# A grouped convolution and a routed low-rank layer on one core: two early tiles in shared blocks, and another order of VectorE's work

## What is computed

```python
out = lax.conv_general_dilated(x, weight, ..., feature_group_count=GROUPS)
out = out + ctx[:, :, None] + bias[None, :, None]        # ctx = c @ c_weight.T
...
base_out = einsum('btd,od->bto', x, base_W) + base_b
probs = softmax(einsum('btd,nd->btn', x, router_W) + router_b)
topk_p, topk_i = lax.top_k(probs, E)
w = sum over the kept routes of topk_p, by expert_map[topk_i]
h = einsum('btd,erd->bter', x, A)
lora = einsum('bter,eor->bto', h * w[..., None], B) * 2.0
result = x_input + base_out + lora
```

## Time and profile before

| | |
|---|---|
| median of three runs | 184.4 us (184.03 to 184.5) |
| the profiled execution, its own time | 184.55 us |
| its span, first to last instruction | 182.7 us |
| PE busy | 178.6 us, 98% |
| DVE busy | 150.9 us, 83% |
| POOL busy | 140.1 us, 77% |
| ACT busy | 81.3 us, 44% |
| transfers | 32.01 MB, 175 GB/s over the span; 362, 382 and 346 GB/s in its second to fourth fortieth |
| granted clock of TensorE | 1.00 |

### The profile page before, as it was taken

How to read it: one execution, slowest core, us unless ns; L and a number is a source line. 1 busy time by engine, 2 the same in 40 slices (tenths; PEclk the granted TensorE clock), 3 DMA queues, 4 the chain that set the end, 5 groups by cost and what they waited for, 6 DMA issues and landing times.

```text
span 182.7 us, 3929 instructions
## 1 busy us (share of the span) xinstructions
PE 178.6 (98%) x1236; PEld 171.3 (94%) x1236; DVE 150.9 (83%) x509; ACT 81.3 (44%) x247; POOL 140.1 (77%) x139
## 2 busy tenths in 40 slices
PE   7999999999999999999999999999999999999993
PEld 3786999999999999999999999999999999999992
DVE  0597899888888889888888988889898889978673
ACT  3657834354544334454433445453344444422320
POOL 2127999999888898888889888888988887885610
PEclk9999999999999999999999999999999999999999
DMA  6999750766475653546475454745635721333304
GB/s 159 362 382 346 251 174 24 218 183 234 155 233 174 185 181 105 170 165 230 134 215 178 140 164 158 229 178 194 182 124 163 256 83 58 98 115 115 118 0 172
DMA packets 17876, 32.01 MB, mean 175 GB/s; under 512 B 1984, under 2 KB 3136, under 8 KB 17856
## 3 DMA queue, kind: packets, MB, share of 16 engines
q1 hardware_dynamic: 17424, 31.40, 52.7%
q10 hardware_dynamic: 432, 0.36, 0.6%
HBM read 23.36 MB, written 8.39 MB: 174 GB/s over the span
## 4 chain that ended last, share of the span: by engine, by line
PE 97%; DVE 1%; issue 0%; POOL 0%; DVEq 0%; POOLq 0%
PE wide_ps L605 61%; PE wide_ps L647 12%; PE conv_banks L591 11%; PE edge_bank L591 3%; PE conv_banks L605 2%; PE odd_bank L634 2%; PE wide_ps L553 1%; PE conv_banks L662 1%; PE conv_banks L564 1%; PE conv_banks L562 1%; DVE xr L978 1%; PE edge_bank L620 0%; PE conv_banks L647 0%; PE edge_bank L634 0%; POOL zeros L462 0%
## 5 line engine op out<-in xcount | busy, mean ns | idle before, releaser
L605 PE MATMUL wide_ps<-wide_hi,y_hi 128*128 128x400 f32 (+1 forms) x248 | 65.7, 325 | 0.0
L605 PE MATMUL wide_ps<-wide_lo,y_hi 128*128 128x400 f32 (+1 forms) x248 | 62.6, 313 | 0.0
L605 PE MATMUL wide_ps<-wide_hi,y_lo 128*128 128x400 f32 (+1 forms) x248 | 62.5, 312 | 0.0
L485 POOL TENSOR_TENSOR terms_lo<-terms,terms_hi 128x512 fp32r<-128x512 f32 x28 | 36.3, 1296 | 18.1 <-ACT terms_hi L385 18.0
L605 PEld LDWEIGHTS wide_ps<-wide_lo,y_hi 128*128 128x128 f32 x248 | 45.9, 188 | 0.2 <-DVE wide_lo L883 0.2
L605 PEld LDWEIGHTS wide_ps<-wide_hi,y_hi 128*128 128x128 f32 x248 | 43.9, 188 | 2.2 <-ACT y_hi L400 0.6
L605 PEld LDWEIGHTS wide_ps<-wide_hi,y_lo 128*128 128x128 f32 x248 | 45.8, 188 | 0.1
L503 POOL TENSOR_TENSOR y_lo<-y,y_hi 128x512 fp32r<-128x512 f32 x31 | 40.2, 1297 | 6.0 <-ACT y_hi L400 6.0
L480 POOL TENSOR_TENSOR xr<-xr,base_b_sb 128x512 f32<-128x512 f32 x32 | 41.5, 1300 | 0.0
L407 ACT ACTIVATE hw_hi<-odd_bank 128x128 fp32r<-128x128 f32 x31 | 8.6, 278 | 53.7 <-PE odd_bank L634 53.6
L780 DVE TENSOR_TENSOR xr<-wide_ps,xr 128x512 f32<-128x512 f32 x30 | 20.7, 691 | 5.2 <-PE wide_ps L647 3.6
(11 more groups left out here) (90 smaller groups left out, 308.9 us busy)
## 6 DMA issues: line engine op xcount, KB each, us to landing
xr<-x_rows SPq DMA_DIRECT2D x32, 256.0 KB, 3.6
out<-xr SPq DMA_DIRECT2D x31, 256.0 KB, 3.2
terms<-x_units SPq DMA_DIRECT2D x28, 256.0 KB, 2.9
edges<-x_edges SPq DMA_DIRECT2D x14, 256.0 KB, 3.1
wide_sb<-wide_w SPq DMA_DIRECT2D x4, 328.0 KB, 4.6
x_in<-x_first SPq DMA_DIRECT2D x3, 264.0 KB, 4.4
weights_sb<-conv_w SPq DMA_DIRECT2D x2, 192.0 KB, 5.3
x_in<-x_first SPq DMA_DIRECT2D x2, 132.0 KB, 2.8
```

The source lines that it names most:

```text
L485: nc.gpsimd.tensor_tensor(terms_lo[i % 2][:, :, :, :], terms[i][:, :, :, :], terms_hi[i % 2][:, :, :, :].bitcast(F32), ALU.subtract)\
L605: mm = nc.tensor.matmul(sums_of(t, k)[:, b, 0:columns[1] - columns[0]], a[k % 2][:, r, :], w[:, r, columns[0]:columns[1]], start=r == 0 an ...
```

## The change

**Tiles 2 and 3** no longer come as `x_in` but in shared blocks (`first_terms`, two tiles; `first_edges`, their pair), in plain float32: `conv_whole` takes the odd block (L699), the own block after its difference (L702), and for tile 2 the edge (L708), each of 256 columns. The difference of tile 2 and that of the edge are POOL's, after all four pieces of `wide_lo` are ready; that of tile 3 is DVE's, after `mark(0, 0)`. The weights have 12 blocks in place of 14, and their pieces are cut and loaded in another order: SP issues the edge and the last piece of weights ahead of those of tile 3.

**DVE's steps.** `condition` is split: its first two instructions stay at the head of the step, the third is now `reach`, behind `best`. `turn` goes to the end of the step, except for t = 28 and t = 29 (`LATE` = 28), where it stands behind `reach` and ahead of `add_out`. `difference` goes from ahead of `best` to behind `mark`. ACT takes `hw_high` ahead of `y_high` up to step 28. Steps 0 and 1 are written anew. POOL takes `bias_rows(0)` ahead of the first `edge_low`. PE's `conv` waits for the rows of the tile before only ahead of its edge part.

```diff
-W_OWN, W_REACH = (1, 2, 5, 6), (0, 3, 4, 7)
-W_SUM, W_QUARTERS = (8, 9, 11, 12), (10, 13)
-W_ALL = 14
+W_OWN, W_REACH, W_SUM, W_QUARTERS = (1, 2, 4, 7), (0, 3), (9, 10, 5, 8), (11, 6)
+W_ALL = 12
...
             load_conv(2)
-            load_x(2)
+            load_first_terms(0)
             sync.wait_ge(wide_in[0], 16)
+            sync.dma_start(first_edges[:, :, :, :], x_edges[0]).then_inc(first_edges_in, 16)
+            load_conv(4)
+            sync.wait_ge(wide_in[1], 16)
             load_conv(3)
-            load_x(3)
+            load_first_terms(1)
...
-                if up_to_tile(t, TILES - 2):
+                if from_tile(t, LATE + 1) and up_to_tile(t, TILES - 2):
                     y_high(t + 1, k + 1)
...
                 hw_high(t - 1, k - 1)
+                if up_to_tile(t, LATE):
+                    y_high(t + 1, k + 1)
...
             conv_low(0)
+
+            pool.wait_ge(wide_lo_ready, RUNS)
+            pool.wait_ge(first_terms_in[0], 16)
+            nc.gpsimd.tensor_tensor(first_terms[0][:, 0, :, :], first_terms[0][:, 0, :, :],
+                                    first_terms[0][:, 1, :, :], ALU.subtract)\
+                .then_inc(first_difference[0], 1)
+            pool.wait_ge(first_edges_in, 16)
+            nc.gpsimd.tensor_tensor(first_edges[:, 0, :, :], first_edges[:, 0, :, :],
+                                    first_edges[:, 1, :, :], ALU.subtract)\
+                .then_inc(first_edge_ready, 1)
             conv_low(1)
...
                     up_low()
-                    edge_low(p + 2, k // 2)
                     pool.wait_ge(base_b_in, 16)
                     bias_rows(t, k)
+                    edge_low(p + 2, k // 2)
...
-            def conv_later(t):
+            def conv_whole(t):
+
+                i, h = t - FIRST, t % 2
                 pe.wait_ge(y_rows_ready, t - 1)
-                pe.wait_ge(conv_w_in[2], 16)
-                pe.wait_ge(x_loaded[t], 16)
-                conv_first(t)
+                pe.wait_ge(conv_w_in[2 + i], 16)
+                pe.wait_ge(first_terms_in[i], 16)
+                nc.tensor.matmul(conv_ps[:, h, 0, :, :], conv_sb[:, W_SUM[t], :],
+                                 first_terms[i][:, 1, :, :], start=True, stop=True)
+                pe.wait_ge(first_difference[i], 1)
+                mm = nc.tensor.matmul(conv_ps[:, h, 1, :, :], conv_sb[:, W_OWN[t], :],
+                                      first_terms[i][:, 0, :, :], start=True, stop=True)
+                if h == 0:
+
+                    pe.wait_ge(cond_biased, GROUPS)
+                    pe.wait_ge(first_edge_ready, 1)
+                    mm = nc.tensor.matmul(edge_ps, conv_sb[:, W_QUARTERS[t // 2], :],
+                                          first_edges[:, 0, :, :], start=True, stop=True)
+                mm.then_inc(conv_done, 1)
...
                 if up_to_tile(t, TILES - 3):
                     condition(t + 2, (k + 2) % GROUPS, q + (k + 2) // GROUPS)
-                    turn(t + 2, k + 2)
-                    hw_low(t - 1, k - 1)
-                elif t == TILES - 2:
+                if up_to_tile(t, TILES - 2):
                     hw_low(t - 1, k - 1)
...
+                choose(t, k)
+                dve.wait_ge(logits_ready, t + 1)
+                best(t, k)
+                if up_to_tile(t, TILES - 3):
+                    reach(t + 2, (k + 2) % GROUPS)
+                    if from_tile(t, LATE):
+                        turn(t + 2, k + 2)
+                dve.wait_ge(top_ready, t + 1)
+                if up_to_tile(t, TILES - 3):
+                    add_out(t - 1, (k - 1) % UNROLL)
+                mark(t, k)
+                if not from_tile(t, LATE):
+                    difference(t + 4, k)
+                weigh(t, k)
+                if not from_tile(t, LATE):
+                    turn(t + 2, k + 2)
```

More of the change, by code:

```diff
@@ L31 @@
 START = 4
+FIRST = 2
+LATE = 32 - 4
 FIRST_ROWS = (slice(0, Q // 2), slice(Q // 2, Q))
@@ L100, in build @@
         zero_exp = sb("zero_exp", [P, 1])
-        x_in = [sb(f"x_in{i}", [P, Q, BLKI]) for i in range(START)]
+        x_in = [sb(f"x_in{i}", [P, Q, BLKI]) for i in range(FIRST)]
+        first_terms = [sb(f"first_terms{i}", [P, 2, Q, MK]) for i in range(START - FIRST)]
+        first_edges = sb("first_edges", [P, 2, Q, MK])
         terms = [sb(f"terms{i}", [P, 2, Q, MK]) for i in range(URING)]
@@ L156, in build @@
         x_first_in = [sem(f"x_first_in{i}") for i in range(2)]
-        x_loaded = [sem(f"x_loaded{i}") for i in range(START)]
+        x_loaded = [sem(f"x_loaded{i}") for i in range(FIRST)]
+        first_terms_in = [sem(f"first_terms_in{i}") for i in range(START - FIRST)]
+        first_edges_in = sem("first_edges_in")
+        first_difference = [sem(f"first_difference{i}") for i in range(START - FIRST)]
+        first_edge_ready = sem("first_edge_ready")
         cond_summed = sem("cond_summed")
@@ L528, in step @@
                 if t == 1:
+                    bias_rows(t, k)
                     terms_low(t + 4, k)
-                    bias_rows(t, k)
                     edge(p + 3, 1 - k // 2)
@@ L921, in step @@
                 if t == 0:
-                    condition_first(2)
+                    condition(2, 2, 0)
+                    reach(2, 2)
                     turn(2, 2)
+                    hw_low(0, 0)
                     choose(1, 1)
@@ L926, in step @@
                     best(1, 1)
+                    condition(3, 3, 0)
+                    reach(3, 3)
+                    return
+                if t == 1:
+                    add_out(0, 0)
                     dve.wait_ge(top_ready, 2)
                     mark(1, 1)
-                    condition_first(3)
-                    hw_low(0, 0)
-                    return
-                if t == 1:
+                    difference(START + 1, 1)
+                    weigh(1, 1)
                     turn(3, 3)
-                    difference(START + 1, 1)
-                    add_out(0, 0)
-                    weigh(1, 1)
                     return
@@ L957, in step @@
                     return
-                if up_to_tile(t, TILES - 2):
-                    choose(t, k)
-                    dve.wait_ge(logits_ready, t + 1)
-                    if up_to_tile(t, TILES - 5):
-                        difference(t + 4, k)
-                    best(t, k)
-                    dve.wait_ge(top_ready, t + 1)
-                    if up_to_tile(t, TILES - 3):
-                        add_out(t - 1, (k - 1) % UNROLL)
-                    mark(t, k)
-                    weigh(t, k)
+                choose(t, k)
[14 more added lines that the diff above has]
+                    turn(t + 2, k + 2)
             steps_of(step)
```

57 lines of the change are left out of this document (31 added, 26 removed).

## The result

The changed kernel takes **185.54 us** (median of 22 runs; the kernel before took 184.62, also in 22 runs): ratio **1.0049, interval 1.0032 to 1.0066**, that is 0.6 to 1.2 us slower. The forecast was 184.5 with a range up to 185.2; the change is slower, and by more than the range allowed. One of the 22 runs of the changed kernel took 249.6 us at a granted clock of 0.66; the ratio leaves it out.

The account below looks back on a forecast made before the run. PE's own list of work was taken as the bound. Start -0.13 and end +0.25, with tile 2, transfers and middle at 0, added 0.12 to 184.4, giving 184.5 us; own range 184.0 to 184.9, with rivals 183.7 to 185.2.

Parts of the forecast that it names:

- Bound: Whole kernel: PE's list sets the time, 97% of the chain; reordering DVE, ACT or POOL in the middle can only lose.
- Tile 2 saves nothing: Start: tile 1 still starts at 14.53, released by ACT's y_hi, so the lighter work of tile 2 gains nothing.
- Tile 3 and POOL's list: Start: POOL's 1.4 us of extra work delays y_lo, up_lo and edge_lo; tile 2's step starts only 0.13 us earlier.
- The 0.24 that I put on POOL: Start: POOL's conv_lo piece stretched by 0.24 us beside DVE's tile 3 difference; without it the gain would be 0.37.
- Transfers, cost 0: Start: 304 KB more on SP's list, 0.8 us for what comes last, delays nothing needed; upper bound 0.3 us.
- The middle, cost 0: Steady steps: DVE's new order keeps hw 0.7 us ahead of PE; cost 0, gain 0 to 0.2 us.
- The end, t = 29: 0.25: Step 29: reach and turn behind best make hw ready at 172.01, PE 0.25 us late; bounds 0 and 0.4.
- The end, t = 28: no cost: Step 28: the same chain ends at 166.9, ahead of turn_hw(28) at 167.4, so it costs nothing.
- The signs: Trace: tile 1 at 14.53, tile 2's front bank about 21.8, turn_hw(29) gap 0.2 to 0.3, steps 5.1 and 5.5 us.
- rival A: Start: PE doesn't wait for POOL, tile 3's saving of 0.83 us arrives, total 183.7 or 183.5 us; chance 0.2.
- Rival B: Start: DVE's tile 3 difference waits for y_lo(1), starting at 15.97; 0.85 us slower with the end, 185.3; chance 0.17.

Follow-up runs that it names:

- steps_only: Kernel before with its old first tiles, but from step 2 VectorE's and ScalarE's lists as in the changed kernel; 185.11 us, 1.0035.
- steps_late: steps_only with the last steps as in late_fix; 184.36 us, 0.9990.
- pool_light: aligned_late with POOL's differences of tile 2 and the first edge cut to one column in sixteen, rows wrong; 184.46 us, 0.9992.
- late_fix: Changed kernel with add_out(27) ahead of the transpose in step 28 and add_out(28) behind weigh in step 29; 185.06 us, 1.0014.
- pool_lighter: pool_light with POOL's second piece of conv_lo and difference of tile 4's edge cut as well; 183.82 us, 0.9961.
- after_again: The changed kernel built once more, for its spread and another profile; 185.82 us, 1.0064.
- aligned_late: Changed kernel with two unused SBUF strips bringing buffers near their old addresses, and the last steps of late_fix; 184.42 us, 0.9992.

## Why the prediction was wrong, point by point

- **Bound.** That PE's list is the kernel's time was right. That an order in the middle could only lose was right but for 0.15 us, inside the 0 to 0.2 that I allowed: steps_only and steps_late have a middle of 116.6, other kernels with the new steps 116.8.
- **Tile 2 saves nothing.** Right: from the first `wide_lo` to tile 1 5.22 before, 5.21 after, released by `y_hi`.
- **Tile 3 and POOL's list.** The mechanism was right, with the waits in place: PE's front bank of tile 2 was put 0.13 earlier and the trace has 0.05 over tiles 1 to 3. The 0.24 that I put on POOL was a split: VectorE's difference lost 0.39 (0.81 against 0.42) and POOL's `y_lo` 0.18 (1.48 against 1.30). The rows show it in order: the difference, begun at 13.50, ends 0.33 after POOL's piece lets `y_lo` start at 13.98, and `y_lo` then ends late. The Trainium skill (SBUF — State Buffer, "SBUF: two separate sides") has it so: the one that comes first keeps the shared port for a whole instruction. By it the gain was to be nothing rather than 0.13, and that is nearer.
- **Transfers, cost 0.** In after this came out right by luck. I argued that the pieces had 0.5 us or more to spare. The piece of weights for the second `conv_hi` landed so late that ScalarE waited 0.87 us for it in after (1.35 in pool_light), and its split was ready 0.2 us before POOL got there. In the traced execution of late_fix, which has the same start, it was paid: the start took 0.4 us longer than in after, more than the 0.3 that I gave as the bound. The saving was behind two doors, and I had looked at one.
- **The middle, cost 0.** This is the step that failed first: +0.35. I had said myself that I would be wrong altogether if the steps in the middle changed their length. The cover of VectorE's list held; the length changed with the buffers that the diff moves, which I had read in it (14 blocks to 12, `x_in` from four to two) and not costed.
- **ScalarE's order, cost 0 (not costed).** `hw_high` ahead of `y_high` looked free. Step 25 pays 0.16 for it.
- **The end, t = 29: 0.25.** Measured +0.21. The size was about right, the place in time wasn't: `hw(29)` started 163.10 us behind the first `wide_lo` (171.70), where the forecast's 171.66 is 162.35 in the trace of before, and PE was then already late by itself.
- **The end, t = 28: no cost.** Failed, +0.33. I followed the new order to `hw(28)` only. `add_out`, which I had moved behind the transpose in the same breath, releases the bank of the next front bank; the same wait that I had found at 21.85 in the earlier trace rows.
- **The signs.** They were given in the clock of the trace of before, and after's trace runs 0.7 us ahead of it. The front bank of tile 2 stands at 21.17, which by my words ("at 21.2 or before") means rival A; tile 1 stands at 13.81 and not at 14.53. Counted from the first `wide_lo` it is 12.57 in after and 12.54 in before: next to nothing was saved by then. Such signs must be distances within one trace.
- **Rival B** did not come: VectorE's difference of tile 3 started at 13.50, which is 14.2 in the clock of before, not after 15. **Rival A** is what pool_lighter shows, 0.6 us less, once POOL and the weights are both out of the way.

The sum as forecast was -0.13 + 0.25; as measured it is -0.05 + 0.35 + 0.16 + 0.33 + 0.21 = 1.00 (0.98 from the unrounded times). Of the four losses one was priced. Two steps failed that I had put at nothing, the middle and step 28; step 25 I had not costed; and the term of the start came to 0.05 in place of 0.13.

## What to carry to other kernels

For each instruction that an edit moves, list everyone who waits for it and not only the chain you have in mind: a sum into the output also gives a bank free. Where one engine's list is taken for the bound, ask when its inputs land, since two bounds that coincide look like one and removing one brings nothing. When a change alters the size of a buffer, compare the distance between the same products before and after; an unused strip tells in one trace whether addresses matter. And build the version that keeps the good half: here the new steps with the old last ones lost nothing, and the whole change did.

## What the runs showed of the hardware

- The address of the buffers changes the rate of TensorE's products of 400 columns: 181.9 to 182.7 ns in eleven kernels with the old layout or near it, 183.2 to 183.3 in seven with the other. With it the stretch of 22 steps takes 0.3 to 0.5 us longer.
- ScalarE has a pause of about 0.28 us at a fixed place of a long unrolled list (step 25), in every kernel with its new order there. It costs nothing in front of idle time and 0.16 to 0.24 in front of an instruction that TensorE waits for. A fetch of instructions would fit. The page lists such transfers, and the trace times them: one of 8 KB starts 0.64 to 0.68 us behind the late `hw_hi` in after, after_again and aligned_late. No run shows that it is the reason:

```profile
q8 instruction: 10, 0.16, 0.4%
q14 instruction: 10, 0.08, 0.2%
```

- VectorE with two inputs in SBUF and GpSimd hold each other up, in both directions: 3.09 us become 4.17, and 0.74 become 1.33.
- Transfers land at different times from one execution to the next. In the profiled execution of late_fix the same piece of weights was split at 12.68 us, 0.27 later than in after when both are counted from the first `wide_lo`; VectorE waited 0.41 us for the block of tile 3; and the start took 0.4 us longer than in after. ScalarE, then VectorE:

```profile
12.68 0.53 ACT L365 ACTIVATE conv_hi<-weights_sb 128x384 fp32r<-128x384 f32 x1 [1.20 <-DMA weights_sb<-conv_w]
```

```profile
13.97 0.46 DVE L955 TENSOR_TENSOR first_terms<-first_terms 128x256 f32<-128x256 f32 x1 [0.41 <-DMA first_terms<-x_units]
```
